# A perceiver layer on one core: the context projection in 18 matmul slots, two batches ahead, with four rotating banks

## What is computed

```python
q = (layernorm(x) @ Wq + bq)       # 64 batches, 32 queries, 16 heads of 16
k = (ctx @ Wk + bk)                # 257 keys from 192 channels
v = (ctx @ Wv + bv)
attn = softmax(clip(q @ k.T * 0.25, -1e4, 1e4))
x = x + (attn @ v) @ Wo + bo       # cross attention
x = x + attention_over_t(layernorm(x))      # 64 time steps, causal
x = x + top2_of_8_experts(layernorm(x))     # gated feed-forward
```

## Time and profile before

| | |
|---|---|
| median of 3 runs | 615.2 us (614.94 to 615.36) |
| span of the profiled execution, first to last instruction | 612.6 us (its time outside the span is not recorded) |
| TensorE matmuls | 594.5 us busy, 97% of the span |
| TensorE weight loads | 484.0 us, 79% |
| VectorE | 457.4 us, 75% |
| ScalarE | 342.2 us, 56% |
| GpSimd | 320.5 us, 52% |
| mean granted TensorE clock | 0.994 of 2.4 GHz |

### The profile page before, as it was taken

The page is one execution under the profiler, slowest core; times in us unless marked ns, Lnnn a source line. Parts: engine busy times, 40 slices in busy tenths (PEclk is TensorE's granted clock), DMA queues, the critical chain, the costliest instruction groups (busy, mean ns, idle before and its releaser), DMA issues.

```text
span 612.6 us, 21666 instructions
## 1 busy us (share of the span) xinstructions
PE 594.5 (97%) x8367; PEld 484.0 (79%) x8367; DVE 457.4 (75%) x1069; ACT 342.2 (56%) x751; POOL 320.5 (52%) x474
## 2 busy tenths in 40 slices
PE   8999999999999999999999999998999999999797
PEld 3788878888788888888888688885588888885675
DVE  4588867888678886777777677689788888884563
ACT  3577868888588888578777255545423333330221
POOL 3456867788677787578874322111333333313771
PEclk9999999999999999999999999998999999999999
DMA  9625453776554845783510598057433334433784
GB/s 233 171 54 128 138 179 105 234 166 208 144 175 134 252 124 194 187 261 102 182 38 3 223 427 333 29 197 231 156 129 130 130 134 142 136 113 120 225 260 135
DMA packets 66069, 102.10 MB, mean 167 GB/s; under 512 B 15505, under 2 KB 42193, under 8 KB 65073
## 3 DMA queue, kind: packets, MB, share of 16 engines
q1 hardware_dynamic: 60672, 86.42, 44.3%
q0 software_dynamic: 4432, 13.50, 7.8%
q10 hardware_dynamic: 864, 0.79, 0.6%
HBM read 69.42 MB, written 31.26 MB: 164 GB/s over the span
## 4 chain that ended last, share of the span: by engine, by line
PE 44%; POOL 26%; issue 17%; DVE 8%; DMA 2%; ACT 1%; POOLq 1%; DVEq 0%; ACTq 0%
PE bank L1932 12%; PE scores L1932 6%; POOL hA L718 5%; POOL lA L714 4%; POOL hA L710 4%; POOL cg L1764 4%; PE bank L1049 4%; PE bank L1042 3%; PE bank L1072 3%; POOL Mb L751 2%; PE scores L1061 2%; POOL tm L742 2%; PE bank L1088 2%; POOL whl L781 2%; PE bank L1957 1%
## 5 line engine op out<-in xcount | busy, mean ns | idle before, releaser
L848 DVE TENSOR_SCALAR Pm<-scores 128x514 f32<-128x514 f32 x128 | 88.1, 688 | 57.2 <-PE scores L1061 57.1
L964 ACT ACTIVATE Pm<-Pm,nm 128x257 f32<-128x257 f32 x256 | 115.8, 505 | 2.5 <-DVE nm L853 2.5
L853 DVE TENSOR_REDUCE nm<-Pm 128x2 f32<-128x514 f32 x128 | 87.5, 684 | 2.2
L1753 POOL DMA_INDIRECT Xg<-y_d,inv x39 | 37.2, 953 | 83.2 <-PE scores L1917 70.0
L959 ACT ACTIVATE PT<-bank 128x512 f32<-128x512 f32 x64 | 38.3, 598 | 74.8 <-PE bank L1072 74.8
L1042 PE MATMUL bank<-hA,wH 128*128 128x258 f32 x256 | 75.3, 305 | 0.1
L1049 PE MATMUL bank<-wH,hA 128*128 128x256 f32 x256 | 74.3, 301 | 0.5 <-DVE PT L860 0.5
L1072 PE MATMUL bank<-cst,Pm 128*128 128x128 f32 x512 | 69.9, 279 | 0.0
L1042 PE MATMUL bank<-hA,wL 128*128 128x258 f32 x256 | 69.1, 281 | 0.0
L1049 PE MATMUL bank<-wL,hA 128*128 128x256 f32 x256 | 68.9, 280 | 0.0
L1891 ACT ACTIVATE sg<-sg 128x512 f32<-128x512 f32 x39 | 24.7, 632 | 77.7 <-DVE sg L1778 77.7
(11 more groups left out here) (280 smaller groups left out, 1432.7 us busy)
## 6 DMA issues: line engine op xcount, KB each, us to landing
w_d<-whl SPq DMA_DIRECT2D x64, 256.0 KB, 3.4
W<-w_d SPq DMA_DIRECT2D x6, 2048.0 KB, 16.4
g_d<-gg SPq DMA_DIRECT2D x39, 256.0 KB, 2.4
wst<-in_W1T SPq DMA_DIRECT2D x32, 256.0 KB, 3.6
cx<-in_ctxT SPq DMA_DIRECT2D x31, 258.0 KB, 3.0
cx<-in_ctxT SPq DMA_DIRECT2D x62, 129.0 KB, 3.5
bb<-in_b SPq DMA_DIRECT2D x8, 512.0 KB, 6.4
W<-w_d SPq DMA_DIRECT2D x5, 512.0 KB, 5.4
```

Of the source, the lines that this page charges most:

```text
L848: v.tensor_scalar(Pm[:, i % 2, 2 * p:2 * p + 2, :], S4[:, 2 * p:2 * p + 2, 0:NK], -CLAMP, CLAMP, ALU.max, ALU.min).then_inc(s_cl, 1)
L853: v.tensor_reduce(nm[:, i % 2, 2 * p:2 * p + 2], Pm[:, i % 2, 2 * p:2 * p + 2, :], AX.X, ALU.max, negate=True).then_inc(s_nm, 1)
L964: a.activation(Pm[:, i % 2, g, :], Pm[:, i % 2, g, :], ACT.Exp, bias=nm[:, i % 2, g:g + 1]).then_inc(s_ex, 1)
L1753: g.indirect_dma_start(out=Xg[:, i % 3, :], out_offset=None, in_=y_d, in_offset=bass.IndirectOffsetOnAxis(ap=inv[:, i:i + 1], axis=0)).the ...
```

## The change

In the second channel group the remainder gets a tile of its own, `lB`, on both halves of the partitions, and `hA` keeps the high part on both. `wL` holds the high weights on rows 0 to 63 and the low ones on rows 64 to 127, so that one 128-row product gives high by high plus high by low. Low by high is left: four products of 64 rows, of which the first and third use rows 0 to 63 and the second and fourth rows 64 to 127. They are issued last, as a pair for K and a pair for V.

The banks 4 to 7 rotate, V takes two banks, and the weighing writes into columns 272 to 339 of the fourth scores bank; new waits keep scores(i) behind total(i-3) and the second clip behind weigh(i-2). The projections of batch i+2 stand at the end of iteration i, behind the query work. ScalarE's order is K out, V out, first turned bank, two exponentials, expert weights, two exponentials. GpSimd's low parts move to odd iterations and its high parts to even ones. The expert weights' high part is made in two halves, in two iterations.

```diff
-        pO = B[7]
+        pO = S4[:, 3, 272:272 + 4 * VH]
-            return B[4 + spot[key] % 3]
+            return B[4 + spot[key] % 4]
...
                     else:
                         g.wait_ge(s_lo, 2 * j + 1)
-                        g.tensor_tensor(hA[64:128, b, 1, :, :], cx[64:128, b, 1, :, :],
-                                        hA[64:128, b, 1, :, :].bitcast(F32), ALU.subtract).then_inc(s_lo, 1)
+                        g.tensor_tensor(lB[:, b, :, :], cx[:, b, 1, :, :], hA[:, b, 1, :, :].bitcast(F32), ALU.subtract
+                                        ).then_inc(s_lo, 1)
...
-                    j, n = (i + 3) // 2 if i % 2 else (i + 2) // 2, 0 if i % 2 else 2
+                    j, n = (i + 3) // 2 if i % 2 else (i + 4) // 2, 2 if i % 2 else 0
...
-                v.tensor_tensor(wL[:, :, :], wA[:, :, :], wH[:, :, :].bitcast(F32), ALU.subtract).then_inc(s_wl, 1)
+                v.tensor_tensor(wL[:, 0, :], wA[:, 0, :], wH[:, 0, :].bitcast(F32), ALU.subtract)
+                v.tensor_copy(wL[0:64, 1, :], wH[0:64, 1, :].bitcast(F32))
+                v.tensor_tensor(wL[64:128, 1, :], wA[64:128, 1, :], wH[64:128, 1, :].bitcast(F32), ALU.subtract
+                                ).then_inc(s_wl, 1)
...
                 def clip(i, p):
...
+                    if i >= 2 and p:
+                        v.wait_ge(s_o, i - 1)
...
                 for i in range(-1, T + 1):
+                    if i + 1 < T:
+                        kevac(i + 1, 0)
+                        kevac(i + 1, 1)
+                        vevac(i + 1)
                     if 1 <= i:
                         ptevac(i - 1)
                     if 0 <= i < T:
                         exps(i, 0)
                         exps(i, 1)
-                    if i + 1 < T:
-                        kevac(i + 1, 0)
-                        kevac(i + 1, 1)
...
+                        c = slice(512 * h, 512 * h + 512)
+                        a.activation(whl[q % 2][:, 0, c], wst[q % 2][:, c], ACT.Copy).then_inc(w_h, 1)
...
-                    if n >= 3:
-                        _, s, val = uses[n - 3]
+                    if n >= 4:
+                        _, s, val = uses[n - 4]
...
-                    return [(hi0, wH[:, 0, :]), (hi0, wL[:, 0, :]), (lo0, wH[:, 0, :]),
-                            (hi1, wH[:, 1, :]), (hi1, wL[:, 1, :])]
...
+                    return [(hi0, wH[:, 0, :]), (hi0, wL[:, 0, :]), (lo0, wH[:, 0, :]), (hi1, wL[:, 1, :])]
+
+                def project(i):
+
+                    j, bi = (i // 2) % 2, i % 2
+                    t.wait_ge(s_lo, 2 * (i // 2) + 1)
+                    bk = []
+                    for m in range(2):
+                        bk.append(take("k", i, m))
+                        for e, (c, w) in enumerate(terms(j, bi)):
+                            t.matmul(bk[m][:, 0:NKP], w[:, 128 * m:128 * m + 128], c, start=(e == 0), stop=False)
+                    bv = []
+                    for h in range(2):
+                        bv.append(take("v", i, h))
+                        for e, (x, w) in enumerate(terms(j, bi)):
+                            t.matmul(bv[h][:, 0:C], x[:, 128 * h:128 * h + 128], w[:, C:2 * C], start=(e == 0), stop=False)
+                    t.wait_ge(s_lo, 2 * (i // 2) + 2)
+                    for m in range(2):
+                        r = slice(64 * m, 64 * m + 64)
+                        t.matmul(bk[m][:, 0:NKP], wH[r, 1, 128 * m:128 * m + 128], lB[r, j, bi, :], start=False, stop=True
+                                 ).then_inc(s_k, 1)
+                    for h in range(2):
+                        r = slice(64 * h, 64 * h + 64)
+                        mm = t.matmul(bv[h][:, 0:C], lB[r, j, bi, 128 * h:128 * h + 128], wH[r, 1, C:2 * C], start=False,
+                                      stop=True)
                     mm.then_inc(s_v, 1)
...
                 def scores(i):
...
+                    if i >= 3:
+                        t.wait_ge(s_oa, i - 2)
...
-                    if i >= 1:
+                    if i >= T - 2:
                         t.wait_ge(s_oa, i)
...
-                for i in range(-1, T + 2):
+                for i in range(-2, T + 2):
...
-                    if i + 1 < T:
-                        for p in range(2):
-                            kproj(i + 1, p)
-                        vproj(i + 1)
...
                     if 0 <= i < 48 and i % 16 == 12:
                         qproj(i // 16 + 1)
+                    if i + 2 < T:
+                        project(i + 2)
```

More of the change, by code:

```diff
@@ L83, in build @@
         B = [S4[:, i, :] for i in range(4)]
-        B += [ctx.enter_context(nc.psum_tensor(f"bank{i}", [128, 512], F32)) for i in range(4, 8)]
+        R4 = ctx.enter_context(nc.psum_tensor("bank", [128, 4, 512], F32))
+        B += [R4[:, i, :] for i in range(4)]
         top = [0]
@@ L212, in build @@
         lA = put("lA", [128, 2, 2, NKP], F32R)
+        lB = put("lB", [128, 2, 2, NKP], F32R)
         Vt = put("Vt", [128, T, 4, VH])
@@ L223, in build @@
         gm = cst[:, C_GM:C_GM + 2]
-        pO = B[7]
-        uses = [(("t", 0, k), s_t0e, k + 1) for k in range(2)] + [(("x",), s_vxe, 2)] + [(("q", 0, m), s_qe, m + 1) for m in range(2)]
-        for i in range(-1, T + 1):
+        pO = S4[:, 3, 272:272 + 4 * VH]
+        uses = [(("t", 0, k), s_t0e, k + 1) for k in range(2)] + [(("x", h), s_vxe, 2) for h in range(2)] + [(("q", 0, m), s_qe, m + 1) for m in range(2)]
+        for i in range(-2, T + 1):
             if 1 <= i:
                 uses += [(("p", i - 1, p), s_pte[p], i) for p in range(2)]
-            if i + 1 < T:
-                uses += [(("k", i + 1, p), s_ke, 2 * (i + 1) + p + 1) for p in range(2)]
-            if i + 1 < T:
-                uses += [(("v", i + 1), s_ve, i + 2)]
             if i == 0:
-                uses += [(("b",), s_basee, 1)]
+                uses += [(("b", h), s_basee, 1) for h in range(2)]
             if 0 <= i < 48 and i % 16 == 11:
@@ L239, in build @@
                 uses += [(("q", i // 16 + 1, m), s_qe, 2 * (i // 16 + 1) + m + 1) for m in range(2)]
+            if i + 2 < T:
+                uses += [(("k", i + 2, p), s_ke, 2 * (i + 2) + p + 1) for p in range(2)]
+                uses += [(("v", i + 2, h), s_ve, i + 3) for h in range(2)]
         spot = {u[0]: n for n, u in enumerate(uses)}
         def held(*key):
-            return B[4 + spot[key] % 3]
+            return B[4 + spot[key] % 4]
         def whalves(n):
@@ L840, in base_row @@
                     v.wait_ge(s_base, 1)
-                    v.tensor_tensor(base[:, :], held("b")[:, 0:C], bcc[:, 0, :], ALU.add).then_inc(s_basee, 1)
+                    v.tensor_tensor(base[:, :], held("b", 0)[:, 0:C], bcc[:, 0, :], ALU.add).then_inc(s_basee, 1)
                 def clip(i, p):
@@ L972, in _ @@
                         exps(i, 1)
-                    if i + 1 < T:
-                        kevac(i + 1, 0)
-                        kevac(i + 1, 1)
+                    if 0 <= i < 48 and i % 16 == 11:
+                        qchunk(i // 16 + 1)
+                    q = (i - 7) // 3
+                    h = i % 3 - 1
+                    if h >= 0 and 0 <= q < 2 * E:
+                        if h == 0:
+                            a.wait_ge(w_d[q % 2], 32 * (q // 2 + 1))
+                            if q >= 2:
+                                a.wait_ge(w_s[q % 2], 64 * (q // 2))
+                        c = slice(512 * h, 512 * h + 512)
+                        a.activation(whl[q % 2][:, 0, c], wst[q % 2][:, c], ACT.Copy).then_inc(w_h, 1)
                     if 0 <= i < T:
@@ L978, in _ @@
                         exps(i, 3)
[L979 to L988, removed]
                     if i in (9, 11, 29):
@@ L1034, in terms @@
                     lo0 = lA[:, b, bi, :]
-                    return [(hi0, wH[:, 0, :]), (hi0, wL[:, 0, :]), (lo0, wH[:, 0, :]),
-                            (hi1, wH[:, 1, :]), (hi1, wL[:, 1, :])]
[L1038 to L1048, removed]
-                            mm = t.matmul(b[:, C * c:C * c + C], x[:, 128 * c:128 * c + 128], w[:, C:2 * C],
-                                          start=(e == 0), stop=(e == 4))
+                    return [(hi0, wH[:, 0, :]), (hi0, wL[:, 0, :]), (lo0, wH[:, 0, :]), (hi1, wL[:, 1, :])]
[21 more added lines that the diff above has]
+                                      stop=True)
@@ L1104, in _ @@
                 t.wait_ge(s_w, 16 * 8)
-                b = take("x")
+                b = take("x", 0)
                 for k in range(2):
@@ L1115, in base_row @@
                     t.wait_ge(s_w3, 16 * 2)
-                    b = take("b")
+                    b = take("b", 0)
                     for k in range(2):
```

18 lines of the change are left out of this document (9 added, 9 removed).

## The result

The changed kernel takes 631.98 us (628.44 to 638.51, 4 runs) beside 615.07 us (614.84 to 615.36, 4 runs) for the kernel before: a ratio of 1.0246, 95% interval 1.0206 to 1.0287. The ratio and its interval leave out the slowest run, 638.51, whose granted clock was lower (0.973 against 0.985 to 0.988). The forecast of 608.9 us had the sign wrong, and the time lies outside 600 to 620.

A forecast was written before the change was run, and what follows sets the result against it. TensorE's order of work was taken to set the cross attention's 4.77 us period, plus a 0.10 us bank wait. 59 x -0.146 = -8.6, +2.6, -0.6, +0.3 give -6.3: 615.2 to 608.9 us, range 600 to 620.

The forecast's parts named there:

- Part 4: GpSimd's splits, SP's renumbered waits and ScalarE's halved conversion in the cross attention: costed at nothing, 0 to 2 us.
- The rival of a new wait: Cross attention: total(i-3) ahead of scores, or GpSimd's weight halves, replaces the old wait; 614 to 616 us, chance 14%.
- Part 1: Projection products: 16 full ones and two half-row pairs for 20; block 0.627 us for 0.673, gaining 0.046 a batch.
- Part 2: Four rotating banks for K and V: the 0.10 us wait for V's bank in each batch goes.
- Part 3: Weighing's sums share the fourth scores bank: new waits have 0.5 us of slack, costing nothing in steady state.
- Part 5: Order at both ends of cross attention: +2.6 us at batch 3, -0.6 at the end, +0.1 each in batches 11, 27, 43.
- 606 to 612: Whole kernel: the reach in us of the forecast's own case, centred on 608.9, given 50%.
- the sum: Whole kernel: steady-loop gain of 8.6 us and the changes at the ends added up to -6.3 us.
- the list of things I costed at nothing: GpSimd's split order and weight halves in the cross attention: a few stalls of 0.3 us, 0 to 2 us together.

The follow-up runs named there:

- the last run: The run with GpSimd's additions later, plus SP's eight residual reloads spread over pairs 25 to 28: 628.09 us beside 634.37 for the kernel before, ratio 0.9899.

## Why the prediction was wrong

**The step that failed** stands at the end of Part 4: "ScalarE's conversion in halves adds one start each time, hidden by its idle time", and ahead of it "SP's waits are renumbered to the same points of time". I priced the moved instruction by its own duration and looked for what is queued behind it, but not for what it waits for. It has a partner on another queue, SP's load, whose pace point the change leaves where it was. The consumer moves: it ran 0.60 us into iteration 9 + 3q, and its first half now has its turn 3.28 us into iteration 7 + 3q, some 6.9 us earlier, the second half some 2.1 us earlier. An engine that is 55% busy hides a longer instruction; it does not hide one that waits, since the other exponentials and the evacuations of the next batch stand behind it in order. The runs put a number on it: 20.4 us between the changed kernel and the one with the halves one iteration later, and 2.5 us ahead of the kernel before with the load alone moved.

The sentence on SP was wrong as well, in a smaller way. The point that means "K of the next batch is made" was 3.6 us into the iteration by the records' ends and is now at its end, 4.6 us in, since the half-row products close both K banks. I don't know what that costs by itself; no run moved it alone.

**The rival of a new wait named the wrong places.** It said 614 to 616 us and stood on total(i-3) or on GpSimd's weight halves. The wait of the scores for VectorE's add is seen once, at the very end (1.84 us, batch 63), and GpSimd holds batches 49 and 50 by a transfer, not by a weight half.

**Part 1, the pairs: right.** Built 0.627 us, measured 0.64; worth 0.046, measured 0.05 with full rows in their place (a single run). They run side by side as argued (0.24 a batch more when they can't), and a switch of tile shape has the price that the start of the kernel showed. By the Trainium skill, "TensorEngine Tiling (Array Packing)", section Key Properties, changing the mode drains the engine; the trace agrees, with 0.21 from the last full product to the first half-row one, where a product in a stream costs 0.12. The Trainium skill's "up to 2x", in the same page's section Theoretical Speedup, agrees with the pairs alone, 0.12 each and 0.24 on the same rows; the block of four products gains 0.05 of 0.47.

**Part 2, the bank: right.** The 0.10 is gone. Periods of 4.65 to 4.66 are 0.12 to 0.13 under before's mean of 4.78, and the forecast was 0.146: a V product stream costs the same, the block 0.013 more, the rest is spread over the slots.

**Part 3: right in the steady loop**, which shows no stall from the shared bank.

**Part 5: sizes off.** Batch 3 starts 3.2 us later (36.17 against 33.00), forecast +2.6; the first scores alone start 3.0 later (21.58 against 18.56), forecast 2.5; the wait of the first V for the base row's copy is there, 1.15 us by the trace. Scores(63) follow scores(62) after 4.22, forecast 4.15. The query iterations cost nothing extra (5.53 = 4.66 + 0.87); I had said 0.1 each. With the halves one iteration later the kernel takes 611.7, at the edge of 606 to 612. At the last scores it is 3.3 us ahead of the kernel before, where the sum said 6.3: some 1.0 us is missing in the loop, 1.5 in batches 49 and 50, 0.5 at the start. So the sum had the right terms with half the gain, and a term of +20 was missing from it.

**Batches 49 and 50** were in the list of things I costed at nothing, 0 to 2 us. They cost 1.5 us with the halves one iteration later and 4.2 with the conversion back; in the changed kernel, where the eighth stall falls on them too, 3.7 and 5.4 in the two traces. The cause is the same kind of thing, and only the last run removes it: the splits ask for a pair's context one iteration earlier than before, and in pair 25 SP issues eight reloads ahead of that load.

## What to carry to other kernels

When an instruction moves to an earlier place in an in-order queue, list what it waits for as carefully as what waits for it, in particular transfers that a pacing scheme issues at fixed points: write down issue, landing and use of each in iterations, and move the issue too. Stalls at a regular distance (here six batches: a piece every three, loads paced by pairs of batches) are found by printing the period of each iteration, not by busy shares. Two pairs of half-height tiles in place of four full products saved two slots, 0.24 us, less one drain and one exposed load, 0.20; put all such work of an iteration in one block.

## What the runs showed of the hardware

A pair of 64x128 float32r products costs one slot, 0.12 us, when the row halves differ, and two when they don't. A trip to half rows and back in the middle of full-size work costs 0.39 us with the pair split off, some three full products. Loads of 256 KB landed 2.6 to 6.1 us after their issue within one execution of the changed kernel, and the second load of piece 10 4.1 us after it with the halves one iteration later and 6.1 in the changed kernel. SP issues that piece behind the loads of `Vt` and the context; that these are the reason is not shown.

Two of the chips ran the kernel before in 634 us and not in 615. The cross attention is not the place: the kernel before with the early conversion ran on such a chip, and its batches without a stall take 4.77 to 4.79 there too. From the last scores' start to the end are 298 to 301 us in the traces of these chips and 279 to 280 in the others. Their profiles show waits in the last stage whose releaser is no engine of this core, as in this one of the last run:

```profile
DVE fo L1808 <- remote: 15.2, 1, 15.2
ACT zT L1913 <- remote: 8.6, 1, 8.6
```

What it is stays open. A ratio to the kernel before on the same chip and the start of the last scores both stand apart from it.
